# The two fp16 halves of a recurrent state, made by two VectorE instructions in place of one

## The reference

```python
def _gru_dir(xp, whh, bhh, reverse):
    h0 = jnp.zeros((xp.shape[0], hid), xp.dtype)
    def step(h, xt):
        gh = h @ whh.T + bhh
        xr, xz, xn = jnp.split(xt, 3, axis=-1)
        hr, hz, hn = jnp.split(gh, 3, axis=-1)
        r = jax.nn.sigmoid(xr + hr)
        z = jax.nn.sigmoid(xz + hz)
        n = jnp.tanh(xn + r * hn)
        h_new = (1.0 - z) * n + z * h
        return (h_new, h_new)
    _, ys = jax.lax.scan(step, h0, jnp.swapaxes(xp, 0, 1), reverse=reverse)
    return jnp.swapaxes(ys, 0, 1)
...
z = seq @ in_w.T + in_b
yf = _gru_dir(z @ gru_wih_f.T + gru_bih_f, gru_whh_f, gru_bhh_f, False)
yb = _gru_dir(z @ gru_wih_b.T + gru_bih_b, gru_whh_b, gru_bhh_b, True)
y = jnp.concatenate([yf, yb], axis=-1) @ out_w.T + out_b
return x + y.reshape(Bx, Hx, Wx, C)
```

## Time and profile before

| | us |
|---|---|
| median of three runs | 1680.24 (1679.62 to 1682.0) |
| the profiled execution | 1683.49 |
| its span, first to last instruction | 1681.7 |
| TensorE matmuls busy | 1612.0 |
| VectorE busy | 1450.3 |
| ScalarE busy | 1162.8 |
| granted TensorE clock, mean over the span | 0.519 of full speed |

### The profile page before, as it was taken

The page is one execution under the profiler, slowest core; times in us unless marked ns, Lnnn a source line. Parts: engine busy times, 40 slices in busy tenths (PEclk is TensorE's granted clock), DMA queues, the critical chain, the costliest instruction groups (busy, mean ns, idle before and its releaser), DMA issues.

```text
span 1681.7 us, 61485 instructions
## 1 busy us (share of the span) xinstructions
PE 1612.0 (96%) x21687; PEld 1230.9 (73%) x21687; DVE 1450.3 (86%) x9046; ACT 1162.8 (69%) x6241; POOL 49.6 (3%) x123
## 2 busy tenths in 40 slices
PE   5899999999999999999999999999999999999997
PEld 5777777777777777777777777777777777777775
DVE  7889999888888888888888888888888888888887
ACT  6866666666666666666666666666666666666666
POOL 5500000000000000000000000000000000000000
PEclk9755555555555555555555555555555555555555
DMA  5200000000000000000000000000000000000000
GB/s 179 74 12 15 12 15 12 12 15 12 13 13 12 14 12 12 14 12 15 12 12 8 12 15 12 14 14 12 15 12 14 13 12 14 13 13 13 12 13 17
DMA packets 40360, 31.29 MB, mean 19 GB/s; under 512 B 3576, under 2 KB 37880, under 8 KB 40056
## 3 DMA queue, kind: packets, MB, share of 16 engines
q1 hardware_dynamic: 40056, 27.35, 5.6%
HBM read 18.95 MB, written 8.39 MB: 16 GB/s over the span
## 4 chain that ended last, share of the span: by engine, by line
DVE 69%; ACT 21%; issue 7%; DMA 1%; PE 1%; POOL 0%; SPq 0%; DVEq 0%
DVE state L904 30%; ACT drive L509 20%; DVE bank L893 18%; DVE halves L913 12%; DVE big L885 3%; DVE seq L869 2%; DVE xin L885 1%; DVE stats L760 1%; DMA xin<-in_x 1%; DVE drive L920 1%; DVE weighted L784 0%; POOL xin L387 0%; DMA gamma_row<-in_gamma 0%; DVE moments L764 0%; PE bank L539 0%
## 5 line engine op out<-in xcount | busy, mean ns | idle before, releaser
L627 PEld LDWEIGHTS bank<-halves,wsplit 128*128 128x128 f16 x18432 | 653.6, 106 | 393.9 <-DVE halves L913 287.3
L627 PE MATMUL bank<-halves,wsplit 128*128 128x16 f16 x18432 | 839.5, 181 | 39.9 <-DVE halves L913 36.4
L904 DVE TENSOR_TENSOR_SCAN state<-gain,drive 128x48 f32<-128x48 f32 x2048 | 526.1, 257 | 172.1 <-ACT drive L509 40.9
L627 PE MATMUL bank<-seq,wcomb 128*128 128x128 f32 x1536 | 592.9, 482 | 2.2 <-DVE seq L869 2.2
L509 ACT ACTIVATE drive<-bank 128x16 f32<-128x16 f32 x2048 | 396.1, 193 | 270.0 <-DVE bank L893 2.2
L503 ACT ACTIVATE rpair<-bank 128x16 f32<-128x16 f32 x2048 | 381.0, 186 | 221.5 <-PE bank L627 221.5
L893 DVE TENSOR_TENSOR_SCAN bank<-rpair,bank 128x32 f32<-128x32 f32 x2048 | 454.4, 222 | 3.4 <-ACT rpair L503 3.4
L913 DVE SCALAR_TENSOR_TENSOR halves<-state 128x32 f16<-128x32 f32 x2048 | 398.4, 195 | 35.5
L506 ACT ACTIVATE gain<-bank 128x16 f32<-128x16 f32 x2048 | 394.2, 192 | 0.0
L627 PEld LDWEIGHTS bank<-seq,wcomb 128*128 128x128 f32 x1536 | 386.0, 311 | 2.7 <-DVE seq L869 2.7
L920 DVE SCALAR_TENSOR_TENSOR drive<-gain,state 128x16 f32<-128x16 f32 x2046 | 364.8, 178 | 0.0
(11 more groups left out here) (100 smaller groups left out, 222.0 us busy)
## 6 DMA issues: line engine op xcount, KB each, us to landing
xin<-in_x SPq DMA_DIRECT2D x16, 512.0 KB, 3.6
big<-in_x SPq DMA_DIRECT2D x96, 64.0 KB
out<-big SPq DMA_DIRECT2D x96, 64.0 KB
xin<-in_x SPq DMA_DIRECT2D x32, 64.0 KB
out<-xin SPq DMA_DIRECT2D x32, 64.0 KB
wih<-in_wiht SPq DMA_DIRECT2D x2, 384.0 KB
con<-in_consts SPq DMA_DIRECT2D x1, 572.0 KB
whh<-in_whht SPq DMA_DIRECT2D x2, 192.0 KB
```

The costliest lines, as they stand in the source:

```text
L627: return nc.tensor.matmul(o, w, m, start=start, stop=True, skip_group_check=True)
L904: v.tensor_tensor_scan(state[:, d, ring, :], gain[:, e, cols], drive[:, e, cols], 0.0, ALU.mult, ALU.subtract).then_inc(state_ready[d], 1)
```

## The change

`split_state` becomes two instructions of 16 columns, upper half first, each with a semaphore of its own. TensorE waits for the upper half ahead of a step's first matmul and for the lower half ahead of its third, which is the first that reads it.

```diff
-    halves_ready = [sem(f"halves_ready{d}") for d in range(2)]
+    high_ready = [sem(f"high_ready{d}") for d in range(2)]
+    low_ready = [sem(f"low_ready{d}") for d in range(2)]
...
             if base + r > 0:
-                pe.wait_ge(halves_ready[d], base + r)
+                pe.wait_ge(high_ready[d], base + r)
...
             parts = ((0, high), (1, high), (2, low))
-            run(G_R, parts).then_inc(reset_pre[d], 1)
+            run(G_R, parts[:2])
+            if base + r > 0:
+                pe.wait_ge(low_ready[d], base + r)
+            run(G_R, parts[2:]).then_inc(reset_pre[d], 1)
             run(G_N, parts).then_inc(reset_and_hn[d], 1)
...
             dve.wait_ge(state_ready[d], base + (r + 1))
-            slot = r // TB * TB + place(r % TB, d)
-            both = state[:, d, slot::RING - slot, 1::3]
-            v.scalar_tensor_tensor(out=halves[:, e, d, :, :], in0=new[:, :, 2].unsqueeze(1).to_broadcast([P, 2, B]),
-                                   scalar=-BIG, in1=both, op0=ALU.add, op1=ALU.subtract).then_inc(halves_ready[d], 1)
+            v.tensor_scalar(halves[:, e, d, 1, :], new[:, :, 2], -BIG, None, ALU.add).then_inc(high_ready[d], 1)
+            v.scalar_tensor_tensor(out=halves[:, e, d, 0, :], in0=new[:, :, 2], scalar=-BIG, in1=new[:, :, 1],
+                                   op0=ALU.add, op1=ALU.subtract).then_inc(low_ready[d], 1)
```

## The result

The changed kernel takes 1760.1 us (median of four runs, 1759.28 to 1761.03) against 1680.0 before (four runs too, one more than in the table above): ratio 1.0474, 95% interval 1.0456 to 1.0493. The forecast was 1805 within 1750 to 1845, so the direction and the range held, and the point was 45 us too high. The rest of this document looks for these 45 us.

A forecast was written before the change was run, and what follows sets the result against it. The prediction took a loop of latencies, not TensorE, to bound the kernel. It added 0.077 us at direction 1 and 0.045 at direction 0, times 1023.5 turns, 125 us, giving 1805 us within 1750 to 1845.

The forecast's parts named there:

- What bounds the kernel now: Whole kernel: a loop of latencies, 1.551 us a turn, with halves 1 on the path and halves 0 beside it.
- this path has some 0.01 us to spare: Path through TensorE (halves, nine matmuls, reset gate, candidate): candidate 0 could have started at 802.42 and started at 802.43.
- Price of a short instruction: VectorE, direction 1: the pair reaches candidate 0 after 0.192 us where one instruction took 0.115, +0.077 us a turn.
- The row with 0.10 us: VectorE profile row used for the price: hold 0 and the output addition start 0.10 us apart.
- The row with 0.09: VectorE profile row used for the price: two plain 16-column instructions with no wait between them start 0.09 us apart.
- its sum of 1752 us: Whole kernel by the skill page's 77 ns price: hold 1 0.01 us too late, 0.07 a turn, 1752 us.
- At direction 0 there is a cover: State 1 waits for hold 1 and tanh 1; the tanh hides about half of hold 1's 0.09 delay, leaving +0.045 us.
- The bounds: Same sum for the whole kernel: low 0.086 us a turn, 1768 us; high 0.165, 1849 us; given 70%.
- rival (a): VectorE: short instructions cheaper than the rows say, direction 0's cost hidden behind tanh 1; 1716 to 1768 us, 14%.
- What the early upper half gives: TensorE: first two matmuls some 0.02 us sooner, reset gate 0.02 to 0.08 later; covered by VectorE, nothing charged.
- rival (b): TensorE: the third matmul's new wait makes reset gate release candidate 1, 0.05 us more a turn; 1849 to 1880 us, 13%.
- Rival (c): VectorE: not slower, as short instructions overlap until lower half and candidate stand 0.057 us apart; 1680 to 1660 us, 3%.

The follow-up runs named there:

- e3_after_one_wait: The changed kernel with TensorE waiting for both halves ahead of its first matmul, so its early start is taken back: 1760.8 us, ratio 1.0475.

## Why the prediction came out as it did

*What bounds the kernel now.* Right in the main: a loop of latencies with state 1, halves 1, candidate 0, tanh 0 and state 0 in it, and TensorE's 96% no bound. Wrong in one step: "this path has some 0.01 us to spare" was worked out from starts, for candidate 0 alone, and for candidate 1 there was nothing to spare. The reset gates cost the kernel before 0.025 us a turn, as leaving out one matmul in both directions shows.

*Price of a short instruction.* This is the term that was mis-sized. I took 0.095 and 0.097 against 0.115; the runs give 0.087, 0.090 and 0.118, so **+0.059 and not +0.077**. The row with 0.10 us was no clean price: hold 0 had waited there for the update gate. In the changed kernel, where it does not wait, the addition starts 0.07 behind it (802.96 and 803.03 in the timeline; medians of 192 turns, 0.097 before and 0.071 after). The row with 0.09 was the one to take.

Of the Trainium skill's prices, the one that I had weighed (VectorE: DVE Perf Modes, section The TRN2 errata: 77 ns for 16 columns, 94 for 32) is below the measured 87 to 90 ns for 16 columns and 118 for 32, and its sum of 1752 us still ends nearer than mine: both of its prices are too low, and in 2 x 77 - 94 = 60 that cancels, against 59 measured. Another page, Vector Engine (DVE) Microarchitecture Reference, section Measured stream behaviour on trn2, has about 75 ns for an instruction and 1.04 for a column, which makes an estimate of 92 and 108 ns. The measured 87 to 90 agrees with it best for 16 columns, but for 32 it is 10 ns too low, and by it the split would cost 2 x 92 - 108 = 76 ns, as much as by my own rows and 17 more than was measured.

*At direction 0 there is a cover.* The mechanism was right: hold 1 takes the tanh's place, and state 1 is late by what sticks out. The size was 0.045 for a measured 0.021. 0.013 of the difference is the price again, twice. The other 0.010 is the distance from candidate 1 to halves 0 (0.127 before, 0.117 after), which I had carried over: it was long because candidate 1 was held.

*The bounds and rival (a).* Both parts lie below my low bounds, 0.059 under 0.061 and 0.021 under 0.025, because no neighbours were let closer than 0.09 and halves 0 was left where a held candidate had put it. Rival (a) got the interval right and the mechanism half: instructions are cheaper than the rows that I took, but not as cheap as its 0.075, and the cost at direction 0 is not hidden, since state 1 follows hold 1 and not tanh 1. That the measured time lies in the range owes as much to its having been stretched down to 1750 as to the sum.

*What the early upper half gives.* Nothing was charged and nothing was gained, and `e3_after_one_wait` shows it by taking it away. That also disposes of rival (b). Rival (c), not slower, had asked for a distance of 0.057.

Together: 0.059 + 0.021 = 0.080 by the medians, and the turns give 0.075. Means over all turns close the gap: 0.023 from state 0 to state 1, 0.058 from halves 1 to candidate 0, and 0.006 less from candidate 0 to state 0 (0.485 before, 0.479 after). About half of the last comes from the first 128 turns, where it went from 0.505 to 0.480. So of the forecast 0.122, price, cover and this term were 0.047 too much, 48 us a run. Of these, 3 come back, since the two profiled executions differ by 77 us in span and the medians by 80: that makes the 45.

## What to carry to other kernels

In a loop of small instructions count instructions, not columns: splitting one of 32 columns into two of 16 costs 0.06 us on the path, because an instruction costs 0.08 to 0.09 and 16 columns save 0.02, and a consumer that could start a little earlier pays for it only if it is the last to arrive. Judge who paces an instruction by its end as well as its start: if its duration grows as the semaphore comes later, it is held, whatever the view of idle time says. When several loops lie within 2% of each other, shortening one shows little, and lengthening one costs less than its price; test them together as well as alone.

## What the runs showed of the hardware that I had not expected

A VectorE scan can be held by a late semaphore though its recorded start is no later: candidate 1 starts 0.175 us behind state 0 held or not, and takes 220 ns held and 202 not. With the semaphore rising 23 to 46 ns ahead of the recorded start, its duration fell from 229 to 207 ns and its end kept 252 to 253 ns behind the semaphore. And such a late scan did not delay the instructions behind it: with candidate 1 ending at 0.393 or at 0.377 us, upper half 0 ended at 0.468 and 0.467.
